# DVE in place of ACT copies the turned z; x is turned first, then z, in a transformer layer on one Trainium2 core

## What is computed

```
x = x + 0.5 * ffn(ln(x));  x = x + linear_attention(ln(x));  x = x + 0.5 * ffn(ln(x))
x = x + 0.5 * spectral(ln(x))
# softmax attention, 16 heads of 64, per batch b (256 tokens)
q = einsum('qdh,bcd->bhcq', Q, x) * sq;  k = einsum('qdh,bcd->bhcq', K, x) * sq
v = einsum('vdh,bcd->bhcv', V, x) * sv
att = where(causal, einsum('bhcq,bhCq->bhcC', q, k) / 64, -inf)
z = einsum('dvh,bhcv->bcd', W, softmax(att) @ v) * (sqrt(128/64) / 16);  x = x + z
# last sublayer: multiply by a circulant matrix in the frequency domain
x = x + 0.5 * (real(ifft(fft(ln(x)) @ w)) + bias)
```

## Time and profile before

| | |
|---|---|
| device time, median of 3 runs | 1265.42 us (1264.5 to 1266.61) |
| the profiled execution | 1264.62 us |
| its span, first to last instruction | 1262.9 us |
| PE busy | 1193.1 us (94%) |
| DVE busy | 1025.6 us (81%) |
| ACT busy | 1003.5 us (79%) |
| POOL busy | 586.6 us (46%) |

### The profile page before, as it was taken

How to read it: one execution, slowest core, us unless ns; L and a number is a source line. 1 busy time by engine, 2 the same in 40 slices (tenths; PEclk the granted TensorE clock), 3 DMA queues, 4 the chain that set the end, 5 groups by cost and what they waited for, 6 DMA issues and landing times.

```text
span 1262.9 us, 38370 instructions
## 1 busy us (share of the span) xinstructions
PE 1193.1 (94%) x10883; PEld 1040.7 (82%) x10883; DVE 1025.6 (81%) x4877; ACT 1003.5 (79%) x3491; POOL 586.6 (46%) x913
## 2 busy tenths in 40 slices
PE   4699977799999999999999999999999999999996
PEld 3588976678888888888888888888888888888885
DVE  6878879977788888888888888888888888888874
ACT  4866648678888888888888888888888888888884
POOL 4821137725444444444444444444444444444442
PEclk9999989999999999999999999999999999999999
DMA  8000000000000000000000000000000000000000
GB/s 222 1 1 0 1 2 1 1 2 2 3 2 9 0 8 7 1 8 0 8 0 8 0 8 0 8 0 8 0 8 0 8 0 8 0 8 0 9 2 18
DMA packets 14444, 11.81 MB, mean 9 GB/s; under 512 B 852, under 2 KB 12664, under 8 KB 14200
## 3 DMA queue, kind: packets, MB, share of 16 engines
q1 hardware_dynamic: 14240, 11.19, 3.3%
q10 hardware_dynamic: 152, 0.00, 0.0%
HBM read 7.00 MB, written 4.19 MB: 9 GB/s over the span
## 4 chain that ended last, share of the span: by engine, by line
PE 85%; DVE 4%; issue 3%; ACT 2%; POOL 2%; DMA 1%; SPq 1%; POOLq 0%; DVEq 0%; ACTq 0%
PE ps L1158 14%; PE ps L1141 13%; PE ps L1167 10%; PE ps L1127 7%; PE ps L1110 7%; PE ps L1123 6%; PE ps L1111 5%; PE ps L1112 5%; PE ps L1149 2%; PE ps L1148 2%; PE ps L1147 2%; PE ps L988 2%; PE ps L1010 1%; POOL rstd L318 1%; PE ps L1183 1%
## 5 line engine op out<-in xcount | busy, mean ns | idle before, releaser
L816 ACT ACTIVATE pr<-ps,neg_max 128x128 f32<-128x128 f32 (+1 forms) x1024 | 424.8, 430 | 110.7 <-DVE neg_max L538 110.7
L333 POOL TENSOR_TENSOR pr<-pr,rinv 128x256 f32<-128x256 f32 x256 | 157.3, 615 | 517.0 <-DVE rinv L546 517.0
L538 DVE CUSTOM_DVE_ANT_0 ps<-ps,mask 128x128 f32<-128x128 f32 (+1 forms) x1024 | 329.4, 389 | 0.5
L335 POOL TENSOR_TENSOR pr<-pr,rinv 128x512 f32<-128x512 f32 x256 | 266.2, 1040 | 0.0
L553 DVE COPY pT<-ps 128x512 f32<-128x512 f32 x256 | 176.1, 688 | 60.1 <-PE ps L1141 58.6
L816 ACT ACTIVATION_READ_ACCUMULATOR pr<-ps,neg_max 128x1 f32 x1024 | 218.0, 213 | 0.0
L1141 PE MATMUL ps<-ident,pr 128*128 128x128 f32 x1536 | 210.2, 273 | 2.5 <-POOL pr L335 1.1
L1141 PEld LDWEIGHTS ps<-ident,pr 128*128 128x128 f32 x1536 | 179.4, 141 | 21.2 <-POOL pr L335 2.6
L1158 PE MATMUL ps<-pT,space 128*64 128x256 f32 (+1 forms) x2048 | 194.9, 332 | 0.7 <-ACT pT L825 0.5
L1158 PEld LDWEIGHTS ps<-pT,space 128*64 128x64 f32 x2048 | 126.8, 136 | 55.5 <-ACT pT L825 0.7
L1110 PE MATMUL ps<-x_hi,wqk_hi 128*128 128x256 f32 x512 | 168.0, 328 | 2.4 <-issue 1.9
(11 more groups left out here) (188 smaller groups left out, 2637.0 us busy)
## 6 DMA issues: line engine op xcount, KB each, us to landing
out<-x_all SPq DMA_DIRECT2D x16, 256.0 KB, 2.3
x_all<-L_attn_x SPq DMA_DIRECT2D x1, 768.0 KB, 7.0
x_all<-L_attn_x SPq DMA_DIRECT2D x1, 512.0 KB, 5.0
space<-L_attn_Q SPq DMA_DIRECT2D x1, 512.0 KB, 15.2
space<-L_attn_K SPq DMA_DIRECT2D x1, 512.0 KB, 9.4
space<-L_attn_V SPq DMA_DIRECT2D x1, 512.0 KB, 11.1
space<-L_attn_W SPq DMA_DIRECT2D x1, 512.0 KB, 11.5
dft_s<-dft SPq DMA_DIRECT2D x1, 192.0 KB, 2.7
```

What stands on the lines that cost most here:

```text
L333: nc.gpsimd.tensor_tensor(pr[:, buf, :, 0, :], pr[:, buf, :, 0, :], r[:, :, 0:1].to_broadcast([P, 2, P]), ALU.mult)
L335: nc.gpsimd.tensor_tensor(pr[:, buf, :, 1:3, :].rearrange("p h b k -> p h (b k)"), pr[:, buf, :, 1:3, :].rearrange("p h b k -> p h (b k)") ...
L538: last = nc.vector.tensor_tensor_reduce(o, o, mask[:, T - w:T], -1.0, -MASKED, ALU.add, ALU.min, neg_max[:, j, 2 * h + qt:2 * h + qt + 1])
L816: last = nc.scalar.activation(dst, ps[:, BANK_S + 2 * j + h, qt * P:qt * P + w], ACT.Exp, bias=neg_max[:, j, at:at + 1], scale=-1.0, accum ...
```

## The change

DVE copies the turned z in place of ACT, at the same p = 2, between `inv_sum` and `x_low`. PE turns x first and z second. ACT's `x_high` now waits for DVE's copy of z (so that the two are not in BANK_X together), and `x_low` waits for `x_high` alone. At the end of the program, too, DVE copies the turned z of batches 30 and 31.

```diff
             def x_low(b, j):
                 dve.wait_ge(xhi_ready, count(b + 1))
-                if above_0(b - 2):
-                    dve.wait_ge(z_xT_ready, count(b - 2))
                 nc.vector.tensor_tensor(x_lo[:, j, :], ps[:, BANK_X, 0:T], x_hi[:, j, :].bitcast(F32), ALU.subtract).then_inc(xlo_ready, 1)
+
+            def z_xT_out(b, w_after=None):
+                dve.wait_ge(z_tr_done, count(b + 1))
+                if above_0(b):
+                    dve.wait_ge(w_done, count(b + 1 if w_after is None else w_after))
+                nc.vector.tensor_copy(z_xT[:], ps[:, BANK_X, T:2 * T]).then_inc(z_xT_ready, 1)
...
+                    if p == X_TURN and above_0(b - 1):
+                        z_xT_out(b - 2)
                     if p == X_TURN and not last:
                         x_low(b + 1, 1 - jb)
...
             z_norm(B - 2, 1)
+            z_xT_out(B - 2)
             probs_T(B * PAIRS - 1, 1)
...
             z_norm(B - 1, 1)
+            z_xT_out(B - 1, B + 1)
             add_spectral(B - 1, B + 2)
...
             def x_high(b, j):
                 act.wait_ge(tr_done, count(b + (SOFT + 1)))
+                if above_0(b - 2):
+                    act.wait_ge(z_xT_ready, count(b - 2))
...
-            def z_xT_out(b, w_after=None):
-                act.wait_ge(z_tr_done, count(b + 1))
-                if above_0(b):
-                    act.wait_ge(w_done, count(b + 1 if w_after is None else w_after))
-                nc.scalar.copy(z_xT[:], ps[:, BANK_X, T:2 * T]).then_inc(z_xT_ready, 1)
...
                     if p == X_TURN and not last:
                         x_high(b + 1, 1 - jb)
-                    if p == X_TURN and above_0(b - 1):
-                        z_xT_out(b - 2)
...
-            z_xT_out(B - 2)
             probs_T(B * PAIRS - 1, 1)
             last_y_out()
-            z_xT_out(B - 1, B + 1)
...
                     if p == X_TURN:
                         pe.wait_ge(v_ready, count(4 * (b + 1)))
+                        if not last:
+                            x_transpose(b + 1, 1 - jb)
                         if above_0(b - 1):
                             spectral_transpose(b - 2)
-                        if not last:
-                            x_transpose(b + 1, 1 - jb)
```

## The result

The changed kernel takes 1269.51 us (median of 13 executions, 1266.04 to 1271.21), the kernel before 1265.42 us (1263.37 to 1268.27). The ratio is 1.0026, with a 95% interval of 1.0016 to 1.0035: 0.26% slower, some 3.3 us; the two means differ by 3.5 us and the two medians by 4.1. The profiled execution has a span of 1267.8 us, against 1262.9.

The account below looks back on a forecast made before the run. PE was taken to bound the loop (busy 856.08 of 859 us), waiting for x_lo at L1167. Loop 2.24 plus tail 0.05 gave 2.3 us: 1265.4 + 2.3 = 1267.7 us, 0.18% slower, range 1264.4 to 1270.0.

Parts of the forecast that it names:

- PE's wait at L1167: First projection matmul, waiting for x_lo: each 0.01 us x_lo moves later costs PE 0.01 us per batch.
- The bound of 6.4 us: At L1167 PE loses 0.36 (even) and 0.10 (odd) per batch; earlier x_lo gains at most 6.4 us in all.
- The five steps of the chain: Last transpose to x_lo: start of DVE's copy 0.04, copy 0.42, hand-over to ACT 0.10, x_high 0.37, x_low's start 0.03; sum 0.96.
- The loop: x_lo later by 0.04 (even) and 0.12 (odd), 14 times each: 2.24 us longer.
- ACT's lateness: Work behind x_high on ACT starts 0.17 (even) and 0.21 (odd) late, hidden within 0.51 of room before PE's odd scores.
- The tail, +0.05: Program's end: the last copy of z is on the path, taking 0.42 on DVE in place of 0.37.
- The rest of the ends: Batches 30 and 31, outside the loop: counted as nothing, one more place at most.
- step 3: Hand-over from DVE's copy to ACT's x_high, a separate wait: 0.10 taken; the forecast spans 0.08 to 0.13, 1266.9 to 1268.5.
- the cheap step: Rival: ACT's separate wait before x_high costs only 0.03, so +0.3 us, 1265.8; chance 0.20.
- The quicker copy: Rival: DVE's copy runs two columns a step, 0.29 instead of 0.42, so -1.4 us, 1264.0; chance 0.03.
- ACT's relief: Rival: ACT rid of 0.27 us per batch speeds the loop, around -4 us, 1261.5; chance 0.07.
- The longer chain of 1.04: Rival: x_high starts after 0.13 and takes 0.42, x_lo 0.12 and 0.20 late, +4.5 us, 1269.9; chance 0.13.

Follow-up runs that it names:

- The delayed x_low: The kernel before with a one-column DVE memset put just ahead of x_low, copies of z left on ACT; ratio 1.0014.
- the one wait at x_high: The changed kernel with x_high's wait for the transposes dropped, so its wait for DVE's copy of z is carried by the instruction; ratio 0.9999.
- the faster version: The kernel before with x_low waiting for z_xT alone and PE's wait for x_lo at L1167 put last, carried by the weight load; 1262.48 us, ratio 0.9977.
- The kernel with z first: The changed kernel with PE turning z before x again, DVE's copy of z waiting for both transposes; ratio 1.0012.
- the last copies on ACT: The changed kernel with ACT again copying the turned z of batches 30 and 31 at the program's end, loop as changed; ratio 1.0019.

## Why the prediction was right, point by point

The time forecast was 1267.7 us; 1269.51 was measured, within the range, and the two repeats gave 1269.16 and 1267.93. The forecast was +2.3 us; the means of the three series are 2.6 to 3.5 over before. The mechanism was right for the loop; what the sum left out is the clock outside it.

- **PE's wait at L1167 is where the change acts, 0.01 for 0.01.** Shown. The delayed x_low moves no copy and lengthened the loop by 1.1 for 1.3 of lateness; the one wait at x_high gave 1.1 back for 1.1. The bound of 6.4 us for what PE loses there was not passed: the faster version took 4.0, half of it by PE's own wait and not by an earlier x_lo.
- **The five steps of the chain.** From PE to the copy 0.04, the copy 0.42, x_high 0.37: as forecast. The hand-over to x_high was 0.08, not 0.10, and x_low followed at 0.04, not 0.03. Sum 0.95 for 0.96. x_lo came 0.03 and 0.11 later in place of 0.04 and 0.12.
- **The loop.** Forecast +2.24. By the measured chain 14 x (0.03 + 0.11) = 1.96; the four profiles with the changed loop, the transposes in its order, have 860.06 to 860.30, 1.8 to 2.0 above before's.
- **The lag between x_lo and L1167** stayed 0.24 and 0.06, as held fixed. The forecast read the one at a product and the other at a weight load; at the weight load they are 0.21 and 0.06. In the sum both are constants, so that nothing came of it.
- **ACT's lateness is hidden.** The piece behind x_high started 0.16 and 0.20 late, by 0.17 and 0.21 as forecast, and PE waited for no exponentials.
- **The order of the transposes costs nothing.** Right for the loop. The sentence beside it was wrong: with z turned first by the kernel's own rule the copy could *not* have started sooner, since PE still writes x's transposes into the bank that DVE would read, and the program keeps the two apart. The kernel with z first waits for both, and its chain is the same; no run let the two meet.
- **The tail, +0.05.** The last copy and its hand-overs cost that. From the end of the last transposes of z to the bias product it was 1258.28 - 1257.82 = 0.46 before and 1263.16 - 1262.64 = 0.52 after:

```profile
1258.28 0.40 PE L1180 MATMUL ps<-bias_bf,ones_bf 128*128 128x256 bf16 x1 [0.46 <-ACT z_xT L856]
```

```profile
1261.95 0.69 PE L1175 MATMUL ps<-ident,z_xn 128*128 128x128 f32 x2 [3.02 <-DVE z_xn L594]
...
1262.68 0.42 DVE L522 COPY z_xT<-ps 128x256 f32<-128x256 f32 x1 [0.78 <-PE ps L1175]
...
1263.16 0.40 PE L1180 MATMUL ps<-bias_bf,ones_bf 128*128 128x256 bf16 x1 [0.52 <-DVE z_xT L522]
```

- **The rest of the ends, taken as nothing: the term that was mis-sized.** The tail was 1.0 to 1.4 us longer in all three profiles of the changed kernel, because the granted clock fell in it. The forecast took for granted that the clock outside the loop is the same in both kernels. But the two profiles of before happened to have none of that fall, and over all executions the clock accounts for less: at a like clock the changed kernel is 2.1 to 2.8 us longer (table above), at any clock 2.7. So of the 3.4 and 2.6 us of the two repeats the loop is 2.0 and 1.9, and 0.4 of the first lie around the span; the mean clock was lower than before's in the first (0.9883 against 0.9897) and the same in the second (0.9895 against 0.9896), so that the last tenths of the second, well inside its interval, stay without a cause. That the first series is 4.1 us over before by its medians is in part chance.
- **The lower end of the forecast.** With 0.08 in step 3 the sum gives 1265.4 + 1.7 + 0.05 = 1267.1, not 1266.9. The measured hand-over of 0.08 is that lower end.
- **The entry of the loop** is in no term of the sum, rightly. In the first pair of profiles it made 2.2 of the 4.9 us, but the stall (1.35 to 2.81 us over all profiles) and the fall of the clock behind it (about 1.6 us) come and go with the execution. Someone who compared the two spans alone would have put the change at more than twice its price in the loop.

The rivals: the cheap step needed x_high 0.03 behind the copy, and that is about what one wait gives (0.04), with a loop 0.6 over before's. In the kernel as changed the wait is separate and cost 0.08. The quicker copy is out, 0.425 for each of the 32. ACT's relief of 6.4 us in the loop bought nothing. The longer chain of 1.04 did not come: x_hi took 0.37. Its time, 1269.9, lies near the measured one, but for another reason.

**What stays open.** Why the tail's clock falls in some executions. It is not who copies z there, as three kernels show: the delayed x_low and the last copies on ACT have ACT's copies and fall, and the one wait at x_high has DVE's copies and does not. It does not follow the length of the loop either: loops of 858.25 to 858.93 (four profiles) kept the clock, loops of 859.40 to 860.30 (six) lost it, 856.36 and 856.81 lost it too, and 854.30 kept it. What the 13 profiles do show is a matter of time. In the eight that have the fall it begins 47.5 to 48.9 us behind the last mark, and the clock falls once more 13.65 us later, in every one of them. In the five without it only that last fall is there; counted back from it by the same 13.65 us, the place would be 45.9 to 47.1 us behind the mark in four and 49.1 in one, outside those 47.5 to 48.9 each time. So the clock seems to change at moments of its own, and whether one of them meets the idle places of the tail would differ between executions of one kernel. That fits the kernel before, whose executions spread over all classes of the clock, and it would make the tail's fall chance and no price of the change. No run moved the tail alone, and this is not shown.

## What to carry to other kernels

Cost a moved copy by the whole chain that it enters, hand-over by hand-over, and ask of each hand-over whether its wait is carried by the instruction or stands ahead of it: here those 0.04 to 0.15 us decided more than who does the copy, and writing waits so that the late one is carried gave 3.4 us with no work moved. Take work from the engine that is not waited for only if its successor does not then wait for a chain of three. And where spans differ by a few us, split them at marks into loop and ends before explaining them, look at the granted clock of the ends in a second execution, and compare executions of a like clock before calling a difference the change's.

## What the runs showed of the hardware that was not expected

- **A wait's form has a price.** Of several waits of an instruction, the one that is carried costs 0.03 to 0.04 from the releaser's end to the start, on ACT (0.04) and on DVE (0.03); as an instruction of its own ahead it costs 0.08 on ACT and 0.10 to 0.11 on DVE. On PE, a wait on a register instruction with another wait between it and the weight load costs 0.21 from x_lo's end to the weight load; carried by the weight load it is 0.06. On PE the edit changed the order alone; on ACT and DVE it also took one wait away. The Trainium skill, "Perfetto Trace Analysis", section "Identifying Dependency Chains", says that an instruction which waits on several engines may have semaphore instructions inserted; the instruction lists here agree, and the price of one is in the numbers above.
- **The granted clock fell behind idle places of PE, but not each time**: behind 1.92 to 2.65 us of idle at the loop's entry in four profiles, and not behind 1.92 to 2.81 in others. A fall there cost about 1.6 us, and one in the tail 0.8 to 1.5.
- **An engine follows itself faster than another follows it.** DVE's copy starts 0.34 behind the start of its own x_low of 0.42, and ACT's second copy 0.26 behind the first, where a hand-over costs the whole duration and 0.04 or more.
